# Self attention with value products in four 32-column tiles and row sums kept apart, on one Trainium2 core

## The reference

```python
scores = jnp.einsum('bhqd,bhkd->bhqk', q, k) / sqrt(hd) + bias     # causal, with relative bias
attn = jax.nn.softmax(scores, axis=-1)
out = jnp.einsum('bhqk,bhkd->bhqd', attn, v)
return out.transpose(0, 2, 1, 3).reshape(Bq, Tq, D) @ w_out.T + b_out
```

## Time and profile before

| | |
|---|---|
| median of 3 runs | 3009.94 us (3008.6 to 3010.54) |
| profiled execution | 3011.65 us, of which the span of instructions is 3009.9 us |
| granted TensorE clock, mean | 0.956 of 2.4 GHz |
| PE / PEld / DVE / ACT / POOL busy | 91% / 60% / 53% / 41% / 12% of the span |
| self attention, first exponential to last eviction | 477 to 1684 us |
| output stage, first DMA to the last query store | 1688 to 1945 us |

### The profile page before, as it was taken

The page is one execution under the profiler, slowest core; times in us unless marked ns, Lnnn a source line. Parts: engine busy times, 40 slices in busy tenths (PEclk is TensorE's granted clock), DMA queues, the critical chain, the costliest instruction groups (busy, mean ns, idle before and its releaser), DMA issues. The chain is left out here.

```text
span 3009.9 us, 42480 instructions
## 1 busy us (share of the span) xinstructions
PE 2752.3 (91%) x12704; PEld 1812.9 (60%) x12704; DVE 1606.2 (53%) x3868; ACT 1242.8 (41%) x2630; POOL 372.6 (12%) x459
## 2 busy tenths in 40 slices
PE   5689987999999999999999589779969999999998
PEld 4678874444444444444444267557747777777777
DVE  4244437777777777777776266457632221222211
ACT  0032221555555555555555234278833222222222
POOL 0300002000000000000000112178546000000000
PEclk7889996999999999999999899889979999999999
DMA  9344445222222222222220577365431000000000
GB/s 287 72 163 178 171 159 136 64 65 66 65 65 65 65 65 65 65 65 65 65 65 8 124 212 223 137 175 170 139 107 37 29 28 29 1 28 28 28 14 14
DMA packets 133923, 271.62 MB, mean 90 GB/s; under 512 B 33875, under 2 KB 54867, under 8 KB 128192
## 3 DMA queue, kind: packets, MB, share of 16 engines
q1 hardware_dynamic: 128896, 254.17, 29.1%
q0 software_dynamic: 4800, 14.68, 1.7%
HBM read 174.39 MB, written 99.98 MB: 91 GB/s over the span
## 5 line engine op out<-in xcount | busy, mean ns | idle before, releaser
L970 ACT ACTIVATE sa_pr<-sa_st 128x512 f32<-128x512 f32 (+3 forms) x1280 | 611.5, 532 | 567.8 <-DVE sa_st L1033 326.3
L938 PE MATMUL sa_ov<-sa_pr,sa_v 128*33 128x512 f32 (+3 forms) x2560 | 538.6, 542 | 0.0
L1019 DVE TENSOR_REDUCE sa_part<-sa_mp 128x1 f32<-128x512 f32 (+3 forms) x768 | 411.8, 583 | 120.1 <-PE sa_mp L919 117.7
L929 PE MATMUL sa_st<-sa_q,sa_k 97*128 97x512 f32 (+3 forms) x1280 | 439.5, 413 | 24.3 <-ACT sa_pr L970 13.9
L929 PEld LDWEIGHTS sa_st<-sa_q,sa_k 97*128 97x128 f32 x1280 | 217.0, 190 | 323.4 <-ACT sa_pr L970 206.0
L919 PE MATMUL sa_mp<-sa_k,sa_q 96*128 96x512 f32 (+3 forms) x1280 | 373.8, 387 | 23.7 <-DVE sa_mp L997 19.1
L1016 DVE CUSTOM_DVE_ANT_0 sa_mp<-sa_mp,sa_ub 128x512 f32<-128x512 f32 (+3 forms) x512 | 318.0, 663 | 76.3 <-PE sa_mp L919 71.9
L1672 DVE TENSOR_TENSOR ff_hl<-ff_hf,ff_hh 128x512 fp32r<-128x512 f32 x128 | 93.5, 730 | 478.7 <-ACT ff_hh L1654 478.7
L105 PE MATMUL ff_f<-ff_ln_hi,ff_w 128*128 128x512 f32 x1024 | 343.7, 397 | 3.2 <-DVE ff_ln_lo L530 3.2
L1617 PE MATMUL ff_o<-ff_w,ff_hh 128*128 128x512 f32 x1024 | 323.9, 397 | 3.3 <-DVE ff_hl L1672 3.3
L919 PEld LDWEIGHTS sa_mp<-sa_k,sa_q 96*128 96x128 f32 x1280 | 233.5, 194 | 94.2 <-DVE sa_part L1019 23.8
(11 more groups left out here) (186 smaller groups left out, 3266.1 us busy)
## 6 DMA issues: line engine op xcount, KB each, us to landing
sa_q<-scratch_q SPq DMA_DIRECT2D x192, 128.0 KB, 4.3
sa_k<-scratch_k SPq DMA_DIRECT2D x192, 128.0 KB, 4.5
scratch_q<-qkv_qst SPq DMA_DIRECT2D x32, 512.0 KB, 3.0
scratch_k<-qkv_qst SPq DMA_DIRECT2D x32, 512.0 KB, 2.8
scratch_q<-sao_qst SPq DMA_DIRECT2D x32, 512.0 KB, 2.8
ca_q<-scratch_q SPq DMA_DIRECT2D x32, 512.0 KB, 4.3
scratch_v<-qkv_vst SPq DMA_DIRECT2D x8, 1056.0 KB, 5.2
sa_v<-scratch_v SPq DMA_DIRECT2D x16, 528.0 KB, 6.5
```

Of the source, the lines that this page charges most:

```text
L929: pe.matmul(st[bank(u, h)][:, 0:w], ks[n.par][:, h, kb * P:(kb + 1) * P], qs[n.par][:, h, g * GW + c0:(g + 1) * GW], start=True, stop=True ...
L938: last = pe.matmul(ov[64 * h:64 * h + VW, c0:GW], vs[n.par][:, kb, h, :], pr[:, u % 4, h, 0:GW - c0], start=(u in opens), stop=(u in ends))
L970: act.activation(pr[:, u % 4, h, 0:w], st[bank(u, h)][:, 0:w], ACT.Exp, scale=SCALE).then_inc(s["exp"], 1)
L1019: dve.tensor_reduce(to, tile, AX_X, ALU.max).then_inc(s["red"], 1)
```

## The change

In self attention:

- The key blocks of a group are put in pairs (`SELF_PAIRS`). The values of two units are now one piece of work: four float32 matmuls into four 32-column tiles of `sa_ov`, partitions 0 to 31 and 32 to 63 for the two heads of the first block, 64 to 95 and 96 to 127 for those of the second. The two halves are added later. The column of ones is no longer used.
- The row sums: GpSimd adds the exponentials of a group, unit by unit, into `sa_acc` (one instruction for both heads, up to 1,024 elements per partition; 30 additions a step and a small copy), and TensorE multiplies the total by ones (`add_up`, two pairs after the group's end) into a PSUM bank `sa_sm`. For three of the 20 pairs (`SUMMED_BY_MATMUL`) four matmuls with ones take the place of the additions. ScalarE copies `sa_sm` out, SP stores it.
- `sa_pr` holds eight units instead of four; the max products use three single banks instead of two double ones, so `sa_sm` has a bank. The table of max steps is written anew.
- ScalarE waits before an exponential until GpSimd has added the unit that lay in the buffer eight units ago.

In the output stage both halves are loaded (`sao_ot` and `sao_o2`, 1 MB each, again four DMAs), and GpSimd adds them (`join`, four additions of 128x512 for a group) before VectorE multiplies. `join` of groups 0 and 1 stands ahead of the loop, that of group g+2 at the head of slot g, before the bias additions of group g.

The core of the diff:

```diff
-SELF_ORDER = ((0, 2, 3, 1), ...
+SELF_PAIRS = (((0, 1), (3, 2)),
+              ((1, 3), (5, 6), (2, 4), (7, 0)),
+              ((6, 1), (2, 9), (5, 8), (11, 10), (3, 7), (0, 4)),
+              ((0, 4), (5, 1), (14, 15), (10, 7), (6, 13), (8, 11), (9, 12), (2, 3)))
+SUMMED_BY_MATMUL = ((2, 2), (3, 3), (3, 5))
+SUMS_AFTER = 2
...
-    NST = 3
+    NST, NMP, NPR = 3, 3, 8
...
+            def add(n, u):                                   # GpSimd
+                g, _, c0, _, _ = units[u]
+                i = pooled_of[g].index(u)
+                if i == 0:
+                    return
+                tile = acc[g % 2]
+                new = pr[:, u % NPR, :, 0:GW - c0]
+                pool.wait_ge(s["exp"], 2 * NU * n + 2 * u + 3)
+                if i == 1:
+                    first = pr[:, pooled_of[g][0] % NPR]
+                    waits(pool, s["summed"], GB * n + g - 1)
+                    last = pool.tensor_tensor(tile[:, :, c0:GW], first[:, :, c0:GW], new, ALU.add)
...
+                else:
+                    pool.wait_ge(s["added"], added(n, u) - 1)
+                    pool.tensor_tensor(tile[:, :, c0:GW], tile[:, :, c0:GW], new, ALU.add).then_inc(s["added"], 1)
...
             def values(n, u):                                # TensorE
...
-                for h in range(2):
-                    last = pe.matmul(ov[64 * h:64 * h + VW, c0:GW], vs[n.par][:, kb, h, :],
-                                     pr[:, u % 4, h, 0:GW - c0], start=(u in opens), stop=(u in ends))
-                last.then_inc(s["av"], 1)
+                for i in range(2):
+                    _, kb, c0, _, _ = units[u + i]
+                    for h in range(2):
+                        tile = ov[HD * (2 * i + h):HD * (2 * i + h + 1)]
+                        v = vs[n.par][:, kb, h, 0:HD]
+                        if first and c0:
+                            pe.matmul(tile[:, 0:c0], v, zeros[:, 0:c0], start=True, stop=True)
+                        last = pe.matmul(tile[:, c0:GW], v, pr[:, (u + i) % NPR, h, 0:GW - c0], start=first, stop=final)
+                if u in direct:
...
+            def add_up(n, g):
+                pe.wait_ge(s["added"], added(n, pooled_of[g][-1]))
...
+                for h in range(2):
+                    last = pe.matmul(sm[HD * h:HD * (h + 1)], ones[:], acc[g % 2][:, h, :], start=not direct_of[g], stop=True)
+                last.then_inc(s["summed"], 1)
...
             def exponent(n, u):                              # ScalarE
-                waits(act, s["av"], NU * n + u - 2)
+                waits(act, s["av"], NU * n + u - NPR + 2)
+                v = (u - NPR) % NU
+                if v in pooled:
+                    waits(act, s["added"], added(n, v) - (NA if u < NPR else 0))
...
             def load_o(g):                                   # output stage, SP
                 waits(sp, s["lo"], KC * g - KC)
+                for x, t in enumerate((ot, o2)):
+                    for j in range(2):
+                        sp.dma_start(t[2 * HD * j:2 * HD * (j + 1), g.par],
...
+            def join(g):                                     # output stage, GpSimd
+                pool.wait_ge(s[f"o{g.par}"], 64 * g.uses + 64)
+                for c in range(KC):
+                    pool.tensor_tensor(ot[:, g.par, c, :], ot[:, g.par, c, :], o2[:, g.par, c, :], ALU.add)\
+                        .then_inc(s["joined"], 1)
+
+            join(Step(0, 0))
+            join(Step(0, 1))
             pool.wait_ge(s["cols"], ncol)
 
             def slot(g, left):
+                if left >= 2:
+                    join(g + 2)
                 pool.wait_ge(s[f"y{g.par}"], 16 * g.uses + 16)
```

More of the change, by code:

```diff
@@ L723, in self_units @@
     out = []
-    for g, order in enumerate(SELF_ORDER):
+    for g, pairs in enumerate(SELF_PAIRS):
+        order = [kb for pair in pairs for kb in pair]
         assert sorted(order) == list(range(TT * (g + 1))) and order[0] <= TT * g
@@ L800, in emptied, with reduced, added, sums_due @@
         return max(i for i in range(2 * NU) if i % NST == j) - 2 * NU
+    def reduced(a, h):
+        j = 2 * a + h
+        if j >= NMP:
+            return j - NMP
+        return max(i for i in range(2 * NM) if i % NMP == j) - 2 * NM
+    def added(n, u):
+        return NA * n + pooled.index(u) + 1
+    def sums_due(n, u):
+        if u + 1 in sums_at:
+            yield n, sums_at[u + 1]
+        if u + 1 + NU in sums_at and not (isinstance(n.n, int) and n.n == 0):
+            yield n + -1, sums_at[u + 1 + NU]
+    def sums_left():
+        last = Step(N // UNROLL - 1, UNROLL - 1, UNROLL)
+        return [(last, sums_at[u]) for u in sorted(sums_at) if u >= NU]
     def after(n, u, left):
@@ L819, in self_attention @@
         ub = [k.sb(f"{name}_ub{i}", [P, 2, GW]) for i in range(2)]
[L820 removed]
+        pr = k.sb(f"{name}_pr", [P, NPR, 2, GW])
+        acc = [k.sb(f"{name}_acc{i}", [P, 2, GW]) for i in range(2)]
+        ssb = k.sb(f"{name}_ssb", [P, 2, GW])
+        ones = k.sb(f"{name}_ones", [P, HD])
+        zeros = k.sb(f"{name}_zeros", [P, GW])
         part = k.sb(f"{name}_part", [P, 2, KB, NCH])
@@ L825, in self_attention @@
         st = [k.ps(f"{name}_st{i}", [P, GW]) for i in range(NST)]
-        mp = [k.ps(f"{name}_mp{i}", [P, 2, GW]) for i in range(2)]
+        mp = [k.ps(f"{name}_mp{i}", [P, GW]) for i in range(NMP)]
+        sm = k.ps(f"{name}_sm", [P, GW])
         ov = k.ps(f"{name}_ov", [P, GW])
-        s = k.sems(name, "init in0 in1 rest0 rest1 scores bias exp av out st0 st1 chunk held red max row0 row1 row2 row3")
+        s = k.sems(name, "init in0 in1 rest0 rest1 scores bias exp av out st0 st1 chunk held red max row0 row1 row2 row3 added summed sumout ss0 ss1")
         block = k.block()
@@ new lines, in values @@
+                if u in direct:
+                    if u == direct_of[g][0]:
+                        pe.wait_ge(s["sumout"], GB * n + g + 1)
+                    for i in range(2):
+                        c0 = units[u + i][2]
+                        for h in range(2):
+                            last = pe.matmul(sm[HD * (2 * i + h):HD * (2 * i + h + 1), c0:GW], ones[:],
+                                             pr[:, (u + i) % NPR, h, 0:GW - c0], start=(u == direct_of[g][0]),
+                                             stop=(i == 1 and u == direct_of[g][-2]))
@@ L937, in values @@
+                last.then_inc(s["av"], 2)
+            def add_up(n, g):
+                pe.wait_ge(s["added"], added(n, pooled_of[g][-1]))
+                if not direct_of[g]:
+                    pe.wait_ge(s["sumout"], GB * n + g + 1)
+                    for h in range(2):
+                        pe.matmul(sm[HD * (2 + h):HD * (3 + h)], ones[:], zeros[:], start=True, stop=True)
                 for h in range(2):
-                    last = pe.matmul(ov[64 * h:64 * h + VW, c0:GW], vs[n.par][:, kb, h, :],
-                                     pr[:, u % 4, h, 0:GW - c0], start=(u in opens), stop=(u in ends))
@@ L956, in slot @@
                     values(n, u)
-                    values(n, u + 1)
-            run(pe, N, slot)
+                    for m, g in sums_due(n, u):
+                        add_up(m, g)
+            run(pe, N, slot, UNROLL)
+            for n, g in sums_left():
+                add_up(n, g)
         @block.scalar
```

141 lines of the change are left out of this document (92 added, 49 removed), and 3 rows, old and new, of the table SELF_ORDER.

## The result

| | before | changed |
|---|---|---|
| median of 4 runs each, same chip | 3009.27 us (3004.07 to 3010.54) | 3134.3 us (3113.82 to 3149.86) |
| ratio, 95% interval | | 1.0416 [1.0362, 1.0469] |
| span of the profiled execution | 3009.9 us | 3128.4 us |
| granted TensorE clock, mean | 0.956 | 0.928 |
| last eviction of `sa_ov` | 1683.7 us | 1676.8 us |

I forecast 2997 us, with 2920 to 3055 as the range, and gave faster 0.54. The time lies outside the range. Of the 118.5 us that the span grew, self attention gave back 6.9 where I had forecast 106, and the output stage with its start took 127.4 where I had forecast 93. Three quarters of the miss of 132 us are thus in self attention.

What follows compares the result with a forecast made beforehand. TensorE was taken to bound self attention: 66.2 us of work and 8 of stalls in a 74.1 us step. Self attention -106, its end +6, output stage +87 gave -13 us: 2997 us, range 2920 to 3055.

Steps and rivals of the forecast that it cites:

- I keep the 8 us of stalls, 58.9 + 8 = 67 us: Self attention: TensorE needs 58.9 us a step, today's 8 us of stalls stay; 67 us, 7.1 less than before.
- will not shrink: Self attention: max products lose one of four banks, so the 8 us of stalls do not get smaller.
- The sums: Self attention, new TensorE work: 2.6 us matmuls with ones, 3.4 us add_up, 0.2 us zero fill; 6.2 us a step.
- 56 to 58: Self attention: GpSimd's 30 additions take 56 to 58 us a step, which fits under the step.
- The tiles: Self attention: four value tiles run side by side, so value products take 19.7 instead of 33.2 us a step.
- Rival A: Self attention: VectorE, or GpSimd at 65 us, holds the step at 70.5 us; 3049 us in total; chance 0.25.
- B: Output stage: the queue loop does not close, only 15 us lost at its start; 2925 us; chance 0.11.
- C: Both stages do better than priced: step 64 us, output stage loses 65 us; 2931 us; chance 0.15.
- the ring: Output stage: residual, evictions, load, join, bias, next residual wait in turn; 40.0 us against 26.6, +13.4 for each of four passes.
- D: Self attention: four tiles of 128 rows do not fully overlap, 4.1 us a step more; 3058 us; chance 0.03.
- Pass R0 to R1: Output stage, residual of group 0 to that of group 1: 34.9 us against 23.8, +11.
- 22 + 6: Group 0's output-stage residual moves by about 22 us; last additions and sums end self attention 6 us later.

Runs made afterwards that it cites:

- (6): Changed kernel without any row sums, and four instead of three banks for the maxima: 3015.86 us, step 67.3 (undisturbed 65.5).
- (9): Changed kernel without any row sums, with its own three banks for the maxima: 3082.17 us, step 71.7 (undisturbed 67.6).
- (13): Changed kernel, sums taking turns in the maxima's four banks, VectorE copying them out, output-stage bias additions before the join: 2999.45 us, ratio 0.9976 to the kernel before.
- Experiment 12: Kernel before, value products over the right half of a unit's columns except each group's first unit: 2893.21 us (before 3009.03), step 67.3.
- experiment 3: Changed kernel, GpSimd's self-attention additions cut to 64 columns of each head: 3120.74 us, step 73.9 (undisturbed 71.7).
- 4: Changed kernel, VectorE's plain maxima taken over half the columns: 3122.6 us, step 74.6 (undisturbed 70.5).
- Experiments 1: Changed kernel, GpSimd's output-stage bias additions of a group put ahead of the join of group g+2: 3054.72 us (before 3005.84).
- 2: Changed kernel, second half of the value products neither loaded nor joined in the output stage: 3027.14 us (before 3007.61).

## Why the prediction was wrong

Undisturbed steps at full clock, in the order of the argument:

| | us |
|---|---|
| before | 72.9 |
| with the value tiles, without sums, four banks (6) | 65.5 |
| with three banks (9) | 67.6 |
| with the sums, the changed kernel | 71.9 |
| with the sums and four banks (13) | 68.9 |

- **The step that failed** is "I keep the 8 us of stalls, 58.9 + 8 = 67 us". The stalls were not a constant. The value tiles took 13.3 us off TensorE (forecast 13.5) and shortened the step by 7.4, so 5.9 us went into new stalls. Experiment 12 shows the same without the tiles. In a fixed order of scores, maxima, scores and values, TensorE's value products had covered part of the wait for a score bank that ScalarE has to free; with shorter ones TensorE is idle there for 3.6 us a step (experiment 6). In the forecast's own terms the mean step has 74.2 - 58.9 = 15.3 us of stalls where I kept 8.
- **The lost bank** stood in the forecast as a reason why the stalls "will not shrink", at no price. It costs 2.1 us without the sums and 3.0 with them (experiment 13, which differs in the place of the sums too).
- **The sums** on TensorE I priced at 6.2 us; all that they bring adds 4.3 to the step (67.6 to 71.9).
- So 65.5 + 2.1 + 4.3 = 71.9, a gain of 1.0 us where I had 7.1. Even that is lost in the means: 2.3 us lie between mean and undisturbed step in the changed kernel, 1.2 before. The loop's jump is in both; the rest is clock, down to 0.87 in the longest step, and it falls mostly behind the jump. My sum had no term for it in this stage.
- **GpSimd**: 58.3 us a step within my 56 to 58, and no bound (experiment 3). An addition of 1,024 elements, priced at 2.25 us, took 2.38. That VectorE's reductions keep their pace beside it could not show, since GpSimd did nothing in that stretch; the rows of the changed kernel do (682 and 713 ns).
- **The tiles** overlap as the row of cross attention had it: 0.99 us to the next matmul in both the earlier trace rows.
- **Rival A**, a step "bound elsewhere" at 70.5 us and 3049, had the right sign with a chance of 0.25. Its cause was wrong: neither VectorE at 57 nor GpSimd holds the step (experiments 3, 4), and it went further than I allowed. B and C fell with the ring and the step, D with the 0.99 us.
- **The output stage** was forecast in the right place and too small. Pass R0 to R1 has +12.1 (forecast +11). The four passes of the ring have +18.1 each on average (forecast +13.4): in the pass shown, 3.0 us more until the load is issued, 2.1 more until it has landed. R5 to R6 adds 2.4 that I had at nothing. Between the last `sa_ov` eviction and R0 lie 77.8 us instead of 37.3, +40.5 for a forecast of 22 + 6 (the 22 stands above its own terms, 12.7 and 6.4, which make 19.1). Experiments 1 and 2 divide it: 11.3 us without load and join, in which the last copy of the sums stands 8.1 us behind the eviction, 10.4 for the second load and the joins, and 18.7 for the queue order. The granted clock in the ring was 0.81:

```profile
1790.50:1970.00 179.50, 105.29 (x448) 84.18 (x448) 77.46 (x137) 41.89 (x68) 41.30 (x33) 0.81 0.59 164
```

- **The sum**: -6.9 + 40.5 + 12.1 + 72.4 + 2.4 = +120.5 against the span's +118.5; the rest of the program is 2 us shorter. Forecast: -106 + 6 + 22 + 11 + 54 = -13.

What stays open: what makes ScalarE free the score banks late, and so what would win the time back. It waits for VectorE's bias and for TensorE's scores in turn. Relieving VectorE's maxima (1.4), its bias additions (1.5) or GpSimd (0.2) each gave little, and more score banks weren't tried for want of a free one. Experiment 6 also has the changed kernel's orders and eight exponential buffers, whose share in the 7.4 us was not taken apart; experiment 12 has neither.

## What to carry to other kernels

Work taken from an engine that is 98% busy in a hand-written order is worth its full time only if nobody else's latency was hidden behind it; here 55 to 60% arrived. Before pricing such a cut, shorten the same work in the kernel as it is (experiment 12) and look at what comes through. A buffer given to a new resource has a price of its own, and a resource that can take its turn in an existing rotation does not need one. When an engine gets a new task that waits for a load, look at what stands behind it in its queue: swapping two blocks was worth 75 us here. And look at what will run beside the new task: the joins slowed VectorE's normalisation wherever the two met (experiment 1).
